# Two of eight gather passes of a graph network replaced by matmuls with an edge-count matrix

## The chip, the cores and the metric

The kernel runs on one NeuronCore of a Trainium2 chip. The metric is the device time of one execution in microseconds (us), the median of several runs. The core has five engines that run their own instruction streams and meet at semaphores: TensorE (PE in the profile, its weight loads PEld), VectorE (DVE), ScalarE (ACT), GpSimd (POOL) and SyncE (SP). DMA transfers are issued from SP, ACT and POOL queues and run on 16 DMA engines. A lower-case q behind an engine (DVEq) marks work of its instruction sequencer.

## What is computed

A graph of 6250 nodes with 128 features and 100,000 edges (sorted by destination) goes through four residual blocks, each behind a layer norm and a relu:

```
x = x + sage(relu(norm(x)))                                  # layer k=0
x = x + edge-product layer(relu(norm(x)))                    # k=1
h = relu(norm(x));  h = relu(sage(h)) twice; x = x + sage(h) # k=2, 3, 4
x = x + three attention layers(relu(norm(x)))                # k=5, 6, 7

sage(h) = mean over edges into a node of h[src] @ Wl + h @ Wr + bias
        = (segment_sum(h[src], dst) / max(count, 1)) @ Wl + h @ Wr + bias
```

The layers k=2, 3 and 4 use the same edges and no edge data, so all three sum the same neighbours; only h differs.

## The kernel before

Nodes lie in 49 tiles of 128 (X, H, G, T and acc are [128, 49*128] in SBUF, f32), handled in 13 chunks of four tiles. Edges lie in 784 tiles of 128, handled in 98 groups of eight (HT = 8); src_t holds the source node of each edge, one column a tile, and loc_t its destination as a number counted from the tile's first node.

Every layer is one pass over all edges. For an ordinary one (edge_pass, k = 0, 2, 3, 4):

- SP stores the chunks of h to one of two tables in DRAM (store_chunk, L724).
- POOL gathers: per edge tile one indirect DMA fetches 128 rows of 512 bytes from the table into rows (L839), 782 a pass. rows has space for two groups, so group c+2 waits until PE has multiplied group c.
- DVE makes, per group, a one-hot matrix from loc_t (make_onehot, L1665), [128 edges, 8, 128 ranks].
- PE multiplies each tile of rows with its one-hot into PSUM (edge_pass, L1263). The result has features on partitions and up to 128 distinct nodes of the tile as columns.
- DVE adds each result into acc at a column that depends on the data: it loads eight start columns into registers (L1674), and adds (add_group, L1689). Each add waits for the one before it.
- In the first 13 groups the product h @ Wr of each chunk is made beside it (turn_rows L1142, copy_turned L903, multiply_rows L1155, take_product L1657).
- Behind the last group, to_nodes takes acc through ACT copies (L942, L957) and two matmuls a tile (L1180 with Wl, L1188 with a permutation by rank that also divides by the count, held in G), and DVE adds the rest and applies the relu (mean_layer, L1877, L1885).

The next layer's gathers wait for the whole table (table_stored). Nothing sets the order but the program text of each engine and the semaphores. k = 1 has its own loops, and k = 5 to 7 (weighted_pass, gathers at L869, DVE's L1774, L1299 on PE) gather too; in these, DVE also picks attention terms with a register-addressed scalar column (L1969).

## Time and profile before

| | |
|---|---|
| three timed runs | 10985.27, 11006.49 and 11007.10 us, median 11006.49 us |
| profiled execution | span 8897.5 us from its first to its last instruction; no time of its own is given beside the span |
| median of the runs less the span | 2109.0 us, in no view of the profile |
| instructions in the span | 96287 |
| mean granted TensorE clock | 0.645 of full speed |
| busy share of the span | PE 49%, DVE 58%, ACT 15%, POOL 71% |
| DMA | 852.66 MB, mean 96 GB/s |

The span is what the profile's views explain. A busy share is an average over stages. The profile records an f32 matmul as two matmul records. "issue" as the reason of an idle stretch means that the engine waited for nothing that the profile shows. In a timeline, x8 stands for eight instructions that follow each other without a gap, and the number behind the start is the length of all of them.

### The profile page before, as it was taken

To read this page: it belongs to the slowest core of one execution; us is meant where nothing else is said; L and a number is where in the kernel's file an instruction comes from. 1 tells how busy PE (TensorE), PEld (TensorE's weight loads), DVE (VectorE), ACT (ScalarE), POOL (GpSimd) and SP (SyncE) were. 2 spreads that over 40 slices of the span, in tenths; PEclk is the share of its full clock that TensorE was granted. 3 is DMA by queue.
4 is the path that set the end of the run, shared out by engine and by line. 5 is a ranking of instruction groups with operands and counts; after the bars stand their busy time and mean duration, and the time that the engine had idled before them with its cause. 6 is when DMAs were issued, how large, how long until landed. Compare 5 with 4: busy or idle time off the path is not lost.

```text
span 8897.5 us, 96287 instructions
## 1 busy us (share of the span) xinstructions
PE 4351.6 (49%) x25019; PEld 3448.9 (39%) x25019; DVE 5136.5 (58%) x15655; ACT 1373.0 (15%) x2233; POOL 6316.3 (71%) x6609
## 2 busy tenths in 40 slices
PE   5565566665433344333533347454266453473533
PEld 3444433333433344333433334254243452443532
DVE  6876577776433333333433348686379773596844
ACT  6666634333100000000100010000010000100000
POOL 6777477776677767777677757777767777677774
PEclk8777777776655566556655565576565665656765
DMA  6555467775211121111221212332123331223311
GB/s 183 157 155 156 137 194 205 199 200 149 70 52 52 52 60 53 52 52 52 59 53 52 53 49 80 116 115 78 38 68 115 120 90 44 72 82 116 115 53 34
DMA packets 598959, 852.66 MB, mean 96 GB/s; under 512 B 130268, under 2 KB 404941, under 8 KB 597456
## 3 DMA queue, kind: packets, MB, share of 16 engines
q0 software_dynamic: 211168, 413.92, 18.0%
q1 hardware_dynamic: 372748, 381.31, 13.9%
q10 hardware_dynamic: 14688, 53.48, 1.5%
q8 instruction: 127, 2.08, 0.1%
q14 instruction: 228, 1.87, 0.1%
HBM read 652.71 MB, written 195.51 MB: 95 GB/s over the span
## 4 chain that ended last, share of the span: by engine, by line
POOL 70%; issue 24%; DVE 3%; PE 2%; ACT 1%; DMA 1%; SPq 0%; POOLq 0%; ACTq 0%; DVEq 0%
POOL rows L839 41%; POOL rows L869 25%; POOL nd L852 2%; POOL at_first L845 2%; PE PS L1180 1%; POOL acc L886 0%; PE PS L1188 0%; DMA rows<-table,src_t 0%; DVE moments L1615 0%; DVE H L2039 0%; DVE H L2040 0%; DVE H L2038 0%; ACT H L929 0%; DVE H L1877 0%; SPq L587 0%
## 5 line engine op out<-in xcount | busy, mean ns | idle before, releaser
L839 POOL DMA_INDIRECT rows<-table,src_t x3910 | 3728.9, 954 | 1465.9 <-issue 1257.2
L1689 DVE TENSOR_TENSOR acc<-acc,PS 128x128 f32 x5474 | 1555.2, 284 | 2914.0 <-PE PS L1263 1708.4
L869 POOL DMA_INDIRECT rows<-table,src_t x2346 | 2245.2, 957 | 903.4 <-issue 758.1
L1263 PE MATMUL PS<-onehot,rows 128*128 128x128 f32 x6256 | 1411.0, 416 | 2189.1 <-DMA rows<-table,src_t 2174.8
L1263 PEld LDWEIGHTS PS<-onehot,rows 128*128 128x128 f32 x6256 | 1306.5, 318 | 2350.8 <-DMA rows<-table,src_t 2330.2
L1299 PE MATMUL PS<-onehot,rows 128*128 128x128 f32 x3060 | 678.1, 411 | 1145.0 <-DMA rows<-table,src_t 1118.0
L1299 PEld LDWEIGHTS PS<-onehot,rows 128*128 128x128 f32 x3060 | 625.4, 312 | 1191.1 <-DMA rows<-table,src_t 1171.2
L1774 DVE TENSOR_SCALAR onehot<-PS,loc_t,shared 128x128 f32<-128x128 f32 x2346 | 942.6, 403 | 0.3
L942 ACT ACTIVATE rows<-acc 128x128 f32 x343 | 78.0, 297 | 2696.5 <-DVE acc L1689 2691.6
L1665 DVE TENSOR_TENSOR onehot<-PS,loc_t 128x1024 f32<-128x1024 f32 x392 | 476.8, 1217 | 0.6
L1372 PEld LDWEIGHTS PS<-als_bf,onehot 128*128 128x128 bf16 x7056 | 308.3, 119 | 427.4 <-DVE onehot L1957 269.7
L1969 DVE SCALAR_TENSOR_TENSOR H<-iota_row,srchi_t,PS 128x49 f32<-128x49 f32 x2352 | 456.9, 254 | 5.9 <-issue 5.9
L1372 PE MATMUL PS<-als_bf,onehot 128*128 128x49 bf16 x7056 | 347.2, 218 | 164.3 <-DVE onehot L1957 155.4
L1957 DVE TENSOR_SCALAR onehot<-PS,iota_col 128x1024 bf16<-128x1024 f32 x294 | 374.0, 1273 | 3.5 <-PE PS L1362 3.5
L1317 PE MATMUL PS<-ident,G 128*128 128x128 f32 x784 | 179.0, 404 | 316.1 <-DVE G L1805 217.9
L1095 ACT ACTIVATE small<-small 128x49 f32<-128x49 f32 x3 | 0.7, 245 | 2020.0 <-DVE small L2021 2020.0
L1362 PE MATMUL PS<-cut_row,ones_bf 1*128 1x512 bf16 x588 | 302.2, 616 | 11.4 <-DVE nd L1951 11.4
L1309 PE MATMUL PS<-H,mats 128*128 128x512 f32 x392 | 300.6, 912 | 10.5 <-DMA H<-soft_rows 10.5
L1299 PE MATMUL PS<-onehot,H 128*128 128x128 f32 x1632 | 271.8, 337 | 38.2 <-DVE onehot L1774 38.1
L1317 PEld LDWEIGHTS PS<-ident,G 128*128 128x128 f32 x784 | 143.5, 211 | 364.1 <-DVE G L1805 265.9
L1299 PEld LDWEIGHTS PS<-onehot,H 128*128 128x128 f32 x1632 | 265.9, 255 | 44.4 <-issue 44.2
L1805 DVE TENSOR_TENSOR G<-G,rows 128x1024 f32<-128x1024 f32 x98 | 120.0, 1224 | 249.4 <-DMA rows<-table,src_t 246.8
(320 smaller groups left out, 5444.5 us busy)
## 6 DMA issues: line engine op xcount, KB each, us to landing
rows<-table,src_t POOLq DMA_INDIRECT x6256, 2.9
staged<-rows ACTq DMA_DIRECT2D x102, 512.0 KB
H<-staged SPq DMA_DIRECT2D x102, 512.0 KB
soft_rows<-shared SPq DMA_DIRECT2D x196, 256.0 KB
H<-soft_rows SPq DMA_DIRECT2D x98, 512.0 KB, 3.9
prod_rows<-onehot SPq DMA_DIRECT2D x98, 512.0 KB, 5.0
shared<-in_edge_weight SPq DMA_DIRECT2D x195, 256.0 KB, 3.6
G<-in_edge_attr SPq DMA_DIRECT2D x97, 512.0 KB, 6.4
```

The source lines that it names most:

```text
L839: pool.indirect_dma_start(rows[:, h * HT + j, :], None, table[k % 2], at(src_t[:, t:t + 1]))\
L869: pool.indirect_dma_start(rows[:, g % 2 * HT + j, :], None, table[k % 2], at(src_t[:, t:t + 1]))\
L1263: last = mm(window_at(k, c, j), rows[:, r, :], onehot[:, r, :], start=True, stop=True)
L1299: last = mm(PS[:, o:o + D], block[:, j * D:(j + 1) * D], onehot[:, h * HT + j, :], start=True, stop=True)
L1317: last = tr(PS[:, 2048 + j * D:2048 + (j + 1) * D], msg0[:, j * D:(j + 1) * D], ident[:])
L1362: last = mm(bank(q), ones_bf[0:1, :], lo_row[:, q * 512:(q + 1) * 512], start=True, stop=True)
L1372: last = mm(PS[:, o:o + NT], hot_bf[:, h, j, :], als_bf[:, part * NT:(part + 1) * NT], start=(part == 0), stop=(part == 2))
L1665: tt(onehot[:, h * HT:(h + 1) * HT, :], iota_ps.unsqueeze(1).broadcast_to([P, HT, D]), loc_t[:, t:t + HT].unsqueeze(2).broadcast_to([P, HT ...
L1689: tt(at, at, window_at(k, c, j), ALU.add).then_inc(added[h], 1 if j < n - 1 else HT - n + 1)
L1774: return ts(onehot[:, c % 2 * HT + j, :], iota_ps, loc_t[:, t:t + 1], ex_t[:, t:t + 1], ALU.is_equal, ALU.mult)
L1957: ts(hot_bf[:, h, :, :].rearrange("p a b -> p (a b)"), PS[:, h * 1024:(h + 1) * 1024], iota_col[:], None, ALU.is_equal).then_inc(lo_hot[h], 1)
L1969: last = stt(mask[:, j, :], iota_row[:, 0:NT], srchi_t[:, ds(e, 1)], cand[:, j, :], ALU.is_equal, ALU.mult, accum_out=als_t[:, ds(e, 1)])
```

## The change

The layers k = 3 and k = 4 no longer gather (GATHERED = 0, 1, 2, 5, 6, 7; DENSE = 3, 4). Their neighbour sums are matmuls of h with a matrix of edge counts A[src, dst] in f32, kept in DRAM as 98 slabs of 64 destination nodes, each [128, 49*64] (adjacency, 98 x 3136 words a partition, which is 157.4 MB).

The matrix is made during the gather pass of k = 2. The 784 edge tiles and the 784 windows of eight destination nodes are walked together in 1567 steps, one edge tile and one window in each. For a step DVE writes two bf16 matrices: the low 7 bits of the source as one-hot [128, 128], and a mask [128, 392] that is 1 at (source tile, node in window) of the edge. PE opens the target with a 4-column matmul and multiplies the two ([128, 392], bf16) into one of three PSUM banks, adding to what the window has so far, and ACT copies the whole window (49 runs of eight words) into one of two slabs in H after every step. SP stores a finished slab. Which tile, bank and slab a step uses depends on the data: the numbers are worked out by DVE and PE in groups 2 to 11 of the pass (compare_tiles, count_tiles, plan_steps, plan_stores) and loaded into registers 16 (DVE, ACT) or 32 (PE) at a time. The steps begin in group 14 and are spread evenly over the 84 groups left. In this pass PE uses three banks for the edge windows, as in k = 0.

```diff
+DENSE = (3, 4);  GATHERED = (0, 1, 2, 5, 6, 7)
+WN = 8;  MASKW = NT * WN;  WINDOWS = ET;  STEPS = ET + WINDOWS - 1
+SLABW = 64;  SLABS = WINDOWS * WN // SLABW;  SLAB_WORDS = NT * SLABW
+LOAD_REGS = 16;  STEP_FROM = 14;  LEAD = 6;  RING = 8
+UNIT_TILES = 7;  UNITS = NT // UNIT_TILES;  SLOTS = 4
...
# SP
+            def store_slabs():
+                sp.wait_ge(tables_ready, 1)
+                for q in range(SLABS):
+                    done = sp.value_load(sp_table[:, q:q + 1], min_val=9, max_val=STEPS + 1)
+                    sp.wait_ge(evacuated, done)
+                    sp.wait_ge(slabs_moved, 16 * (q + 1))
+                    sp.dma_start(adjacency[:, q * SLAB_WORDS:(q + 1) * SLAB_WORDS], slab(q)).then_inc(slabs_moved, 16)
...
+            def load_units(k):
+                for c in range(NCH):
+                    for u in range(UNITS):
...
+                        elif n >= SLOTS:
+                            sp.wait_ge(units_used, n - SLOTS + 1)
...
+                        sp.dma_start(slot_of(n)[:, 0:nslabs(c)],
+                                     of[:, :, u * UNIT_TILES:(u + 1) * UNIT_TILES, :]).then_inc(units_in[n % SLOTS], 16)
...
# POOL
-            for k in range(K):
+            for k in GATHERED:
...
# ACT
+            def evacuate(i, first):
+                s.wait_ge(stepped, i)
+                s.wait_ge(evacuated, i)
+                to = H[:, ds(first[WN + i % WN], SLAB_WORDS)].rearrange("p (h d) -> p h d", d=SLABW)[:, :, 0:WN]
+                nc.scalar.activation(to, PS[:, ds(first[i % WN], MASKW)].rearrange("p (h d) -> p h d", d=WN), ACT.Copy)\
+                    .then_inc(evacuated, 1)
...
# PE
+            def adjacency_step(i):
+                if i % LOAD_REGS == 0:
+                    pe.load(bank_regs, pe_table[:, 2 * i:2 * (i + LOAD_REGS)])
...
+                wait(pe, evacuated, i - 1)
+                pe.wait_ge(masked, i + 1)
+                mm(PS[:, ds(bank_at[LOAD_REGS + i % LOAD_REGS], 4)], ones_bf[:], zeros_bf[:, 0:4], start=True, stop=True)
+                mm(PS[:, ds(bank_at[i % LOAD_REGS], MASKW)], lo_slot(i), mask_slot(i), start=False, stop=True,
+                   skip_group_check=True).then_inc(stepped, 1)
...
+                        for i in range(steps_by(c - 1), steps_by(c)):
+                            adjacency_step(i)
...
+            def dense_pass(k):
...
+                            last = mm(sums_at(c).rearrange("p (s d) -> p s d", d=SLABW), of[:, t, :],
+                                      slot_of(n)[:, 0:nslabs(c), j, :], start=(t == 0), stop=(t == NT - 1))
+                        last.then_inc(units_used, 1)
...
+                for c in range(NCH):
+                    wait(pe, sums_copied, done + c - 1)
+                    add_units(c, range(0, 2))
+                    turn_rows(k, c)
+                    if c > 0:
+                        means(c - 1)
+                    add_units(c, range(2, 4))
+                    multiply_rows(k, c)
+                    add_units(c, range(4, UNITS))
+                means(NCH - 1)
...
# DVE
+            def mask_step(i):
+                if i % LOAD_REGS == 0:
+                    v.load(tile_regs, dve_table[:, i:i + LOAD_REGS])
...
+                wait(v, stepped, i - RING + 1)
+                ts(lo_slot(i), iota_16[:, 0:D], slo_t[:, ds(t, 1)], None, ALU.is_equal)
+                ts(mask_slot(i), iota_16[:, 0:MASKW], window_cols[:, i:i + 1], key_t[:, ds(t, 1)], ALU.add, ALU.is_equal)\
+                    .then_inc(masked, 1)
...
+                    begun, ended = steps_by(c - 1), steps_by(c)
+                    if c >= STEP_FROM:
+                        masks_to(begun + LEAD)
+                        add_group(2, c, c * HT,
+                                  lambda j: masks_to(begun + LEAD + (ended - begun - LEAD) * (j + 1) // HT))
+                        masks_to(ended)
```

means(c) multiplies the sums of chunk c, copied to SBUF by ACT, with Wl; dense_layer on DVE multiplies with 1/count, adds the product h @ Wr and the bias, and applies the relu (k = 3) or adds x and takes the moments for the next norm (k = 4), chunk by chunk. A unit is [128, 8 slabs, 7 source tiles, 64], 1.84 MB in runs of 1792 bytes; a full chunk needs seven, the last chunk has two slabs instead of eight.

How the pass of k = 2 changes on the engines, in the middle of the pass. DVE before, one group of edges (from the load of the start columns to the one-hot of group c+2):

```order
L1674 TENSOR_LOAD seg_row
L1675 ISA
L1689 ISA [waits added1,multiplied0]
L1689 TENSOR_TENSOR acc<-acc,PS 128x128
L1689 ISA [waits added0]
L1689 TENSOR_TENSOR acc<-acc,PS 128x128
```

and DVE now, the same place (L1925 is the add, L2068 the one-hot of the source, in bn, and L2069 the mask, in shared or cut_row):

```order
L1925 ISA [waits added1]
L1925 TENSOR_TENSOR acc<-acc,PS 128x128
L2068 ISA [waits stepped]
L2068 TENSOR_SCALAR bn<-work,shared 128x128
L2069 ISA
L2069 TENSOR_SCALAR shared<-work,GT,shared 128x392
L2068 ISA [waits stepped]
L2068 TENSOR_SCALAR bn<-work,shared 128x128
L2069 ISA
L2069 TENSOR_SCALAR shared<-work,GT,shared 128x392
```

Between two adds there now stand two or three steps of two operations each, and each step waits until PE has done the one eight before.

PE now, at the seam between the steps of one group and the edge matmuls of the next (L1452 is the line that was L1263, RO the rows and one-hots); before, only the rows of L1263 stood here:

```order
L1432 MATMUL PS<-cut_row,bn 128x392
L1452 MATMUL PS<-RO 128x128 [waits added1,onehot_ready1,gathered1]
L1452 MATMUL PS<-RO 128x128 x3
L1452 MATMUL PS<-RO 128x128 [waits added0]
L1452 MATMUL PS<-RO 128x128 x3
L1431 ISA [waits masked,evacuated]
L1431 MATMUL PS<-work,ones_bf 128x4
L1432 ISA
L1432 MATMUL PS<-cut_row,bn 128x392
L1431 ISA [waits masked,evacuated]
```

The eight edge matmuls of a group stand in one block, and no step runs on PE while they do.

ACT now, where it takes up the next eight steps (ACT had no instruction in this part of the pass before):

```order
L1099 ACTIVATE H<-PS 128x49x8
L1108 TENSOR_LOAD GT
L1109 ISA
L1110 ISA
L1111 TENSOR_LOAD GT
L1111 ISA x2
L1099 ISA [waits evacuated,stepped,slabs_moved]
L1099 ACTIVATE H<-PS 128x49x8
L1099 ISA [waits evacuated,stepped]
```

Every copy waits for its own predecessor (evacuated) and for PE (stepped); every eighth has two register loads before it, and a wait for a stored slab.

Listed row by row (rows that repeat folded), the five engines' programs have 24195 rows before and 37593 now.

## Rows read from the trace of the kernel before

**Rows 1.** Page: the chain that ended last, shares of the span by engine.

```profile
POOL 70%; issue 24%; DVE 3%; PE 2%; ACT 1%; DMA 1%; SPq 0%; POOLq 0%; ACTq 0%; DVEq 0%
```

**Rows 2.** Chain in order of time (start, length): table stores before k = 2, 3, 5.

```profile
2256.16 2.10 DMA table<-H
...
3276.87 1.93 DMA table<-H
...
5349.09 2.32 DMA table<-H
```

**Rows 3.** Timeline of k = 3 from 3511.8 us (start, length, engine, line).

```profile
3511.81 3.78 PE L1263 MATMUL PS<-onehot,rows 128*128 128x128 f32 x16 [6.19 <-DMA rows<-table,src_t]
3513.01 0.94 POOL L839 DMA_INDIRECT rows<-table,src_t  x1 [0.30 <-issue]
...
3515.72 3.22 DVE L1689 TENSOR_TENSOR acc<-acc,PS 128x128 f32 x8 [5.61 <-PE PS L1263]
...
3518.86 1.22 DVE L1665 TENSOR_TENSOR onehot<-PS,loc_t 128x1024 f32<-128x1024 f32 x1
...
3521.86 3.78 PE L1263 MATMUL PS<-onehot,rows 128*128 128x128 f32 x16 [6.26 <-DMA rows<-table,src_t]
```

**Rows 4.** Stages (start:end, us, busy of PE, PEld, DVE, ACT, POOL, clock, DMA share, GB/s).

```profile
3244.00:3279.00 35.00, 27.22 (x208) 26.47 (x208) 18.16 (x39) 18.43 (x62) 0.95 (x1) 0.84 0.34 96
3279.00:4265.00 986.00, 383.21 (x1700) 357.04 (x1700) 345.71 (x883) 7.44 (x13) 736.96 (x782) 0.60 0.20 52
```

**Rows 5.** Groups by line and shape: ScalarE PSUM copy, VectorE scalar op in SBUF.

```profile
L957 ACT ACTIVATE onehot<-PS 128x512 f32<-128x512 f32 x84 | 49.7, 592 | 30.4 <-PE PS L1180 30.3
...
L1003 ACT ACTIVATE H<-PS,bias_cols 128x1024 f32<-128x1024 f32 x98 | 109.3, 1115 | 613.5 <-PE PS L1309 613.5
...
L1885 DVE TENSOR_SCALAR H<-H 128x512 f32<-128x512 f32 x24 | 10.2, 426 | 0.8
```

**Rows 6.** Register loads (8 and 4 registers) and register arithmetic: ns min/median/max.

```profile
L1674 DVEq TENSOR_LOAD <-seg_row x686: 593/596/1094, 61.1 to 8816.8; - x172
...
L1675 DVEq FUSED_REGOPS  x686: 157/189/195, 62.0 to 8817.5; - x172
...
L938 ACTq TENSOR_LOAD <-rank_row x91: 293/310/912, 1050.2 to 8842.5; - x91
```

**Rows 7.** Timeline, TensorE at the end of k = 7 and its loads at 303 us.

```profile
8825.47 1.06 PE L1188 MATMUL PS<-onehot,G 128*128 128x128 f32 x8
8826.36 1.06 PE L1180 MATMUL PS<-gat_wa,rows 128*128 128x128 f32 x8
...
303.69 0.19 PEld L1247 LDWEIGHTS PS<-shared,mats 128*128 128x128 f32 x1 [0.24 <-issue]
304.12 0.19 PEld L1247 LDWEIGHTS PS<-shared,mats 128*128 128x128 f32 x1 [0.24 <-issue]
```

**Rows 8.** Timeline, VectorE in k = 5: adds and weights in turn, then picks.

```profile
5984.09 0.40 DVE L1774 TENSOR_SCALAR onehot<-PS,loc_t,shared 128x128 f32<-128x128 f32 x1
5984.41 0.28 DVE L1689 TENSOR_TENSOR acc<-acc,PS 128x128 f32 x1
...
5440.48 0.25 DVE L1969 SCALAR_TENSOR_TENSOR H<-iota_row,srchi_t,PS 128x49 f32<-128x49 f32 x1
...
5440.67 0.25 DVE L1969 SCALAR_TENSOR_TENSOR H<-iota_row,srchi_t,PS 128x49 f32<-128x49 f32 x1
```

**Rows 9.** Timeline, gathers and VectorE casts within SBUF in k = 0.

```profile
102.91 1.30 POOL L839 DMA_INDIRECT rows<-table,src_t  x1 [0.30 <-issue]
106.13 0.94 POOL L839 DMA_INDIRECT rows<-table,src_t  x1 [0.30 <-issue]
...
102.83 0.57 DVE L1493 CAST G<-G 128x784 bf16<-128x784 f32 x1
```

**Rows 10.** DMA from 1500 to 1520 us: GB/s in 40 slices of 0.5 us, packets.

```profile
GB/s 66 229 360 373 327 347 353 283 277 335 349 268 104 16 131 0 131 0 0 238 66 139 401 346 343 348 389 295 296 327 365 288 117 0 131 0 41 90 0 131
DMA packets 4957, 4.15 MB, mean 208 GB/s; under 512 B 354, under 2 KB 4450, under 8 KB 4957
```

More of the change, by code:

```diff
@@ L79 @@
 SAGE = (0, 2, 3, 4)
+DENSE = (3, 4)
 GAT = (5, 6, 7)
+GATHERED = (0, 1, 2, 5, 6, 7)
+WN = 8
+MASKW = NT * WN
+WINDOWS = ET
+STEPS = ET + WINDOWS - 1
+SLABW = 64
+SLABS = WINDOWS * WN // SLABW
+SLAB_WORDS = NT * SLABW
+LOAD_REGS = 16
+PLAN_FROM = 2
+STEP_FROM = 14
+LEAD = 6
+RING = 8
+UNIT_TILES = 7
+UNITS = NT // UNIT_TILES
+UNIT_WORDS = CW * UNIT_TILES
+SLOTS = 4
+PLANS = -(-(STEPS + 1) // PW)
 def build(nc, a, out):
@@ L1721, in edge_pass, with edge_keys @@
                         first_softplus(p)
+            def edge_keys():
+                dst8, digit, own, first = (scan_tmp(G, i) for i in range(4))
+                v.wait_ge(slabs_moved, 16)
+                step(ts(dst8.bitcast(I32), key_t.bitcast(I32), 3, None, ALU.arith_shift_right))
+                step(ts(digit.bitcast(I32), key_t.bitcast(I32), WN - 1, None, ALU.bitwise_and))
+                step(copy(own, digit.bitcast(I32)))
+                step(copy(first, dst8.bitcast(I32)))
+                step(stt(own, srchi_t[:], float(WN), own, ALU.mult, ALU.add))
+                step(stt(key_t, first, 512.0, own, ALU.mult, ALU.add))
+                step(ts(digit.bitcast(I32), src_t[:], P - 1, None, ALU.bitwise_and))
+                step(copy(slo_t, digit.bitcast(I32)))
@@ new lines, in compare_tiles @@
+            def compare_tiles(p):
+                w = plan_width(p)
+                for b in range(NB):
+                    if p < PLANS:
+                        last = ts(compared(b)[:, 0:w], iota_16[0:TB, 0:w], float(p * PW), tile_end[:, b:b + 1],
+                                  ALU.add, ALU.is_gt)
+                    else:
+                        last = ts(compared(b)[:, 0:w], iota_16[0:TB, 0:w], 8.0, tile_window[:, b:b + 1],
+                                  ALU.mult, ALU.is_gt)
+                step(last, tiles_compared)
@@ new lines, in plan_stores, with plan @@
+            def plan_stores():
+                v.wait_ge(edges_counted, PLANS + 1)
+                sums = only_last
+                row = int_a[0:1, 0:SLABS].bitcast(F32)
+                step(stt(row, iota_16[0:1, 0:SLABS], 8.0, counted_ps[0:1, 0:SLABS], ALU.mult, ALU.add))
+                step(ts(sp_table, row, 9.0, None, ALU.add), tables_ready)
+            def plan(c):
+                if c == 0:
+                    edge_keys()
+                if c == 1:
+                    step_constants()
+                p, rest = divmod(c - PLAN_FROM, 2)
+                if 0 <= p <= PLANS:
+                    if rest == 0:
+                        compare_tiles(p)
+                    elif p < PLANS:
+                        plan_steps(p)
+                    else:
+                        plan_stores()
@@ new lines, in gather_and_build, with masks_to @@
+            def gather_and_build():
+                made = 0
+                def masks_to(n):
+                    nonlocal made
+                    while made < min(n, STEPS):
+                        mask_step(made)
+                        made += 1
+                for c in range(2):
+                    make_onehot(c)
+                for c in range(NG):
+                    begun, ended = steps_by(c - 1), steps_by(c)
[4 more added lines that the diff above has]
+                        masks_to(ended)
+                    else:
+                        add_group(2, c, c * HT)
+                    if c + 2 < NG:
+                        make_onehot(c + 2)
+                    if 1 <= c <= NCH:
+                        take_product(2, c - 1)
+                    plan(c)
@@ new lines, in dense_layer @@
+            def dense_layer(k):
+                done = (k - 3) * NCH
+                for c in range(NCH):
+                    g, x = chunk(acc3 if k == 3 else H3, c), chunk(X3, c)
+                    v.wait_ge(means_ready, done + c + 1)
+                    step(tt(g, as_tiles(means_at(c)), per_node(rcount, c), ALU.mult), means_used)
+                    v.wait_ge(p_product, c + 1 + k * NCH)
+                    tt(g, g, as_tiles(product_at(k, c)), ALU.add).then_inc(p_done, 1)
+                    v.wait_ge(p_done, c + 1 + k * NCH)
+                    step(tt(g, g, vec_nodes(bias_vec[k], len(tiles_of(c))), ALU.add))
+                    if k == 3:
+                        ts(g, g, 0.0, None, ALU.max).then_inc(h_chunks, 1)
+                    else:
+                        step(tt(x, g, x, ALU.add))
+                        row_moments(c)
+                        if c > 0:
+                            shift_rows(c - 1, False)
+                if k == 4:
+                    shift_rows(NCH - 1, False)
```

341 lines of the change are left out of this document (278 added, 63 removed).

## The prediction

> **What bounds the kernel now.** I read the page first. The chain that ended last is POOL for 70% of the span and "issue" for 24% [rows 1]; the reader is to see that no arithmetic engine is in it. The chain in order of time gives the layers' borders, each the landing of the last table chunk [rows 2]: k = 2 runs from 2258.3 to 3278.8 us, 1020.5 us, and k = 3 and 4 together to 5351.4 us, 2072.6 us. Then the timeline inside a pass [rows 3]: a gather is 0.94 us and the next starts 0.30 us later, so a group of eight takes 10.0 us, which is the distance from one TensorE block to the next (3511.81 to 3521.86). In those 10 us TensorE is busy 3.78 us, and DVE 3.22 for the adds and 1.22 for a one-hot. The stages [rows 4] say the same: of the 986 us pass, PE is busy 383, DVE 346, ACT 7, at a granted clock of 0.60. A pass is 98 groups at the pace of POOL, and the others have room beside it.
>
> **What goes.** Two gather passes with their node stages: 2072.6 us.
>
> **What comes in the pass of k = 2.** 1567 steps over 84 groups are 18.65 a group. They are free while each engine's work for a group stays under 10.0 us. I price the engines in turn.
>
> ACT copies 128x392 from PSUM per step. Copies of 512 and 1024 columns took 592 and 1115 ns [rows 5], so about 1.02 ns a column, and 392 make 0.47 us. Each copy waits for its own predecessor before its addresses are made. The adds do the same: eight take 3.22 us and one 0.28 [rows 3, 8], so 0.42 from start to start and 0.14 of it wait. A step is 0.61 us. Every eighth step first loads 16 registers: 8 cost 596 ns and 4 cost 310 [rows 6], so 72 each and 1.17 us for 16; with the arithmetic on them (0.19 for eight, twice), a 17th register and its arithmetic (0.2) it is 1.75 us, of which the copy still running covers 0.47. That leaves 1.3 in eight steps: 0.77 us a step, **14.4 us a group**. Already this is above 10.0.
>
> To it comes the seam. PE's block of eight edge matmuls runs 3.78 us at the low clock [rows 3] and 1.8 us at the high one (four matmuls in 0.89 us [rows 7]); I take 2.8, since the clock was granted to 0.60 [rows 4] and PE will be somewhat busier. When PE turns to the block, ACT has three copies left, 1.8 us. Block, last step and first new step (0.3 us each, from their columns at the high clock) are 3.4 us, so ACT idles 1.6 us. PE's own load of 32 registers (2.3 us, and 0.8 of arithmetic) comes each 16 steps, but ACT has three copies and its own load then, also 3.1 us: nothing. Sum: 16.0 us.
>
> DVE. The picks, whose operand column comes from a register too, follow each other every 0.19 us [rows 8]: a floor of 0.37 us for a step's two operations. The ceiling is one element a cycle with the fixed part of L1774 (0.32 us for 128 columns [rows 8]): 0.32 and 0.60, so 0.92. An operation within SBUF ran faster: 512 columns of four bytes in 426 ns [rows 5] where one a cycle would need 533. If it is bytes that count, the mask's 392 two-byte columns stream in 0.10 us; with 0.19 fixed for each, the pair costs 0.47, which I take as it stands nearest to this row and to the floor. A group is then 8.8 plus eight adds (2.2), one-hot (1.2) and register loads (2.6): 14.8 us. The Trainium skill (VectorE: DVE Perf Modes, "The perf-mode tier table") gives 16-bit scalar operations within SBUF four elements a cycle; no row here shows one, and by it the sum would be the same.
>
> PE: block 2.8, steps about 0.4 each (7.5) and loads 3.6: 13.9 us. POOL: gathers get longer while DVE works within SBUF. Two gathers that met a 0.57 us cast took 1.30 us, not 0.94 [rows 9]: 0.36 more, 0.63 of the cast's length. Of a group's 8.8 us of masks that is 5.5 us, so 15.5 with the 10.0.
>
> The Trainium skill has the rule for it (SBUF — State Buffer, "Who interferes with whom"): two-port VectorE operations and GpSimd exclude each other for the whole instruction. The trace agrees in kind, with 0.36 us of the 0.57; held in full, it is a rival below.
>
> So four chains need 16.0, 15.5, 14.8 and 13.9 us for a group and hand work to each other through rings of three to eight steps. I take **16.5 us**, half a microsecond for their friction, between 13.0 (no load exposed) and 18.8.
>
> The layer k = 2: 14 groups at 10.0 (140); 20 us for the planning in groups 2 to 11 (some 100 small DVE operations of about 0.4 us, mostly beside the gathers; the ends are 0 and 50); 84 x 16.5 = 1386; the node stage, 35 as before [rows 4], and 8 for the last copy and the last slab's store. Together 1589 us, 568 more than before. SP's stores (98 of 1.6 MB) fill the DMA engines only in part: 157 MB in 1.4 ms is 113 GB/s, beside 50 for the gathers.
>
> **What comes as k = 3 and 4.** A full chunk is 49 matmuls of 512 columns. An f32 matmul is two records, and two records of 512 columns start 0.43 us apart [rows 7], so 0.86 us for a matmul; twelve chunks make 506 us. The last chunk of 128 columns takes 49 x 0.22 = 11, and turn, product and means (three more of 128 columns for 49 tiles) 33. That is 550 us at the high clock. Whether it is held: through the end of k = 7 [rows 7] PE ran without a gap at 0.89 us for eight records, the high level; in the passes, with gaps of 6.2 us before each block, a block took 3.78, the low level [rows 3]. A dense layer has no gaps as long as units arrive. A unit is 1.84 MB for seven matmuls, 6.0 us, so 306 GB/s are asked. With 4450 of 4957 packets under 2 KB the engines moved 277 to 401 GB/s in the slices in which they were hardly idle [rows 10]; a unit's 1792-byte runs should do no worse: 5.3 us at the 345 in the middle, and 6.6 at 277, which would make a layer 50 us longer. Four slots cover the rest. I add 10 us a layer for gaps, 8 for the first units, and 15 behind the last chunk until the table of k = 5 has landed (the norm is made chunk by chunk beside the sums). 2 x 560 + 23 = 1143 us, 929.6 less than the 2072.6.
>
> **Sum.** Span 8897.5 + 568 - 930 = 8536 us. Between the span and the runs' median lie 2109 us that no view explains; I leave them as they are, so 11006.5 - 361 = **10645 us**, -3.3%. A change under about 0.2% could not be told from none.
>
> **Rivals.**
> - VectorE sets the pace. At two elements a cycle, as the row of 426 ns has it, a step costs 0.64 and a group 11.9 + 6.0 = 17.9 us: 84 x 1.4 more, 10763 us. At one a cycle 23.2 us, +563: 11208 us, slower. For it: mask operations have two column operands, and L1774 is such. Against: the operations in SBUF show better than one. 0.17, of it 0.05 for the second.
> - POOL sets the pace. If gathers lose the masks' full length, 10.0 + 8.8 = 18.8 us a group, +193: 10838 us. It needs the exclusion to be whole, where rows 9 show 0.36 of 0.57. The rule of the Trainium skill (SBUF — State Buffer, "Who interferes with whom") is this case. 0.12.
> - The other side: units come too slowly in k = 3 and 4. At 200 GB/s, a little under the 208 that rows 10 moved with their idle slices, a unit takes 9.2 us, a layer 793, and the result is 11111 us; if the gaps also drop TensorE to the low level, a matmul takes 1.71 us, a layer 1100, and the result is 11725. It decides from 8.6 us a unit (213 GB/s) on, where the two layers give back the 361. Against it: the full slices of rows 10. For it: the slabs lie 12.5 KB apart within a row, and no row shows such a read. 0.11.
> - It does not do what it says: the 2109 us around the span grow. The programs have 37593 rows and not 24195; if that time goes with them, it grows by 1168 to some 11810 us. No view shows it either way. 0.05.
> - The forecast keeps 0.55, between 10350 (13.0 us groups: 84 x 3.5 less) and 10900.
>
> **Chances.** Faster: the forecast 0.55, VectorE at two a cycle 0.12, POOL 0.12 together 0.79; within 0.2%: 0.03, from the milder end of slow units; slower: 0.18, from slow units (0.08), VectorE at one a cycle (0.05) and the time around (0.05). The range reaches from 10300, a little under the 13.0 us groups, to 11100, which takes in both pace rivals and slow units at their start; the one-a-cycle masks, cold dense layers and a grown surrounding are left out.
>
> **What would show it.** Right: k = 2 takes about 1590 us, with steps of about 0.77 us on ACT beside idle time of 1.6 us a group before the first copy; TENSOR_LOAD on ACT near 1.17 us; PE in k = 3 and 4 at a clock over 0.95, 0.43 us between records, hardly waiting for units. Wrong: POOL without pauses in k = 2 and gathers of 2 us; DVE over 90% busy there; PE in k = 3 waiting for units; or a span that falls while the runs don't.

## The result: slower by 3.2%, and the profile after

| | |
|---|---|
| changed kernel, four runs | 11346.44 to 11361.01 us, median 11352.08 us |
| kernel before, four runs | 10981.07 to 11007.10 us, median 10995.88 us |
| ratio | 1.0321, 95% interval 1.0306 to 1.0335 |
| predicted | 10645 us (10300 to 11100) |
| profiled execution of the changed kernel | 11347.99 us, span 11346.2 us, TensorE clock 0.643 |

The time lies outside the range and on the other side of no change. The first thing to see is the last row: here span and time differ by 2 us. There are no 2109 us around the span, as there seemed to be in the kernel before; experiment e0 takes that up.

Page of the changed kernel: busy shares, three rows of the 40 slices, and the chain (which answers to [rows 1]).

```profile
PE 5627.2 (50%) x27414; PEld 3519.3 (31%) x27414; DVE 5247.5 (46%) x17197; ACT 2131.4 (19%) x3703; POOL 4841.9 (43%) x5045
...
POOL 5666466655222222221000173266570466650664
PEclk7766666666555555556999955566555665555756
...
GB/s 163 136 133 140 141 162 172 162 146 49 81 80 81 81 74 81 85 82 111 297 284 291 238 79 36 52 98 41 56 95 6 93 72 36 75 72 19 101 59 34
...
DVE 2%; POOL 2%; issue 2%; another core or an unknown queue 1%; PE 0%; DVEq 0%; DMA 0%; POOLq 0%; ACT 0%; SPq 0%
```

The chain can't be followed back in this execution (its shares sum to 7%), so the passes have to be measured by their gathers. In the slices, POOL falls to 2 tenths for eight slices (the pass of k = 2), and then TensorE's clock stands at 9 tenths and the DMA engines at 238 to 297 GB/s for four (k = 3 and 4). The second is what was predicted, the first is not.

Changed kernel, POOL's gathers of k = 2 and the first of k = 5: count, duration in ns (min/median/max), first and last start in us.

```profile
L958 POOL DMA_INDIRECT RO<-table,src_t x782: 939/947/1305, 2647.4 to 5258.9; - x196
```

```profile
L988 POOL DMA_INDIRECT RO<-table,src_t x24: 943/947/948, 6470.2 to 6498.9; - x24
```

The pass of k = 2 takes 2612 us (5258.9 + 0.95 - 2647.4), where 140 + 20 + 1386 = 1546 were forecast. From its last gather to the first of k = 5 it is 1210 us, where 43 + 1143 = 1186 were forecast. The dense layers are nearly right and the building of the matrix is not.

Changed kernel, two stages (columns as in [rows 4]): the middle of the pass of k = 2, and the dense layers.

```profile
2800.00:5200.00 2400.00, 1090.50 (x4270) 562.73 (x4268) 958.61 (x3699) 734.38 (x1477) 620.71 (x654) 0.57 0.22 80
5500.00:6000.00 500.00, 495.96 (x1391) 238.90 (x1390) 30.08 (x56) 13.70 (x24) 0.00 (x0) 1.00 0.83 287
```

In the pass nobody is busy for half of the time, so it is no engine's throughput. In the dense layers PE is busy 496 of 500 us at the high clock, with 287 GB/s beside it.

What the pass waits for stands in the timeline at a sixteenth step. Changed kernel, from 3990.7 us (rows of POOL, PEld and most of the others left out):

```profile
3990.82 0.50 PE L1432 MATMUL PS<-cut_row,bn 128*128 128x392 bf16 x1
...
3991.45 0.50 ACT L1099 ACTIVATE H<-PS  x1 [0.19 <-issue]
...
3998.61 0.50 ACT L1099 ACTIVATE H<-PS  x1 [6.66 <-issue]
...
4001.94 0.18 PE L1431 MATMUL PS<-work,ones_bf 3*128 3x4 bf16 x1 [10.62 <-issue]
...
4002.73 0.25 DVE L2068 TENSOR_SCALAR bn<-work,shared 128x128 bf16<-128x128 int16 x1 [8.43 <-PE PS L1432]
...
4002.99 0.50 ACT L1099 ACTIVATE H<-PS  x1 [3.89 <-PE PS L1432]
```

PE stands for 10.6 us and ACT for 6.7, both for "issue", and DVE and ACT then wait for PE. The register loads of this run say why (line 1427 is PE's load of 32 registers, 1108 and 2064 those of 16 on ACT and DVE, 1910 the load of eight start columns that was at L1674; the three numbers are the shortest, the median and the longest, in ns):

```profile
L1427 PEldq TENSOR_LOAD <-GT x98: 7516/10073/10575, 2822.4 to 5305.9; - x98
```

```profile
L1108 ACTq TENSOR_LOAD <-GT x196: 3367/3392/6607, 2809.0 to 5319.4; - x196
```

```profile
L2064 DVEq TENSOR_LOAD <-GT x98: 3582/3594/4121, 2817.9 to 5297.1; - x98
```

```profile
L1910 DVEq TENSOR_LOAD <-seg_row x490: 593/597/1756, 61.4 to 11266.2; - x164
```

By the medians that is 315 ns a register on PE, 212 on ACT and 225 on DVE, where [rows 6] gave 72 to 78. The load of seg_row is still at 75 in this same execution, so it isn't the execution that makes loads slow. The new tables hold 16-bit numbers (`G[0:1, ...].bitcast(U16)`); seg_row and rank_row, on which the price rested, hold 32-bit ones.

### The profile page after: what moved, and what is told of

Same layout as the page of the kernel before. It is cut to its first block and busy times, and to the rows that moved or that the text cites. A ratio compares the mean times of both kernels' runs of the same rounds, so it can differ in the third digit from the quotient of the medians.

```text
span 11346.2 us, 113568 instructions
## 1 busy us (share of the span) xinstructions
PE 5627.2 (50%) x27414; PEld 3519.3 (31%) x27414; DVE 5247.5 (46%) x17197; ACT 2131.4 (19%) x3703; POOL 4841.9 (43%) x5045
## 3 DMA queue, kind: packets, MB, share of 16 engines
q0 software_dynamic: 161120, 311.32, 10.6%
## 5 line engine op out<-in xcount | busy, mean ns | idle before, releaser
L988 POOL DMA_INDIRECT RO<-table,src_t x2346 | 2256.6, 962 | 3367.4 <-DMA table<-H 1287.9
L958 POOL DMA_INDIRECT RO<-table,src_t x2346 | 2242.8, 956 | 2919.5 <-PE PS L1452 1676.6
L1925 DVE TENSOR_TENSOR acc<-acc,PS 128x128 f32 x3910 | 1098.0, 281 | 1674.0 <-remote 1074.8
L1530 PE MATMUL PS<-RO 128*128 128x128 f32 x3060 | 649.1, 398 | 1136.7 <-DMA RO<-table,src_t 776.2
L1099 ACT ACTIVATE H<-PS x1567 | 779.4, 497 | 1716.3 <-issue 977.6
L1603 PE MATMUL PS<-als_bf,RO 128*128 128x49 bf16 x7056 | 397.4, 218 | 1192.5 <-issue 903.2
L1530 PEld LDWEIGHTS PS<-RO 128*128 128x128 f32 x3060 | 602.3, 301 | 1182.8 <-DMA RO<-table,src_t 797.3
L2169 DVE TENSOR_SCALAR RO<-PS,loc_t,shared 128x128 f32<-128x128 f32 x2346 | 943.4, 404 | 0.6
L2068 DVE TENSOR_SCALAR bn<-work,shared 128x128 bf16<-128x128 int16 x1567 | 411.2, 262 | 1123.0 <-PE PS L1432 792.4
L1452 PE MATMUL PS<-RO 128*128 128x128 f32 x3128 | 593.5, 366 | 182.7 <-DMA RO<-table,src_t 97.2
L1452 PEld LDWEIGHTS PS<-RO 128*128 128x128 f32 x3128 | 579.9, 279 | 288.1 <-DMA RO<-table,src_t 132.0
L1490 PE MATMUL PS<-GT,H 128*128 128x512 f32 (+1 forms) x966 | 394.1, 565 | 1.4 <-DMA GT<-adjacency 1.4
L1490 PE MATMUL PS<-GT,acc 128*128 128x512 f32 (+1 forms) x952 | 392.3, 569 | 0.0
```

Of the source, the lines that this page charges most:

```text
L958: pool.indirect_dma_start(rows[:, h * HT + j, :], None, table[k % 2], at(src_t[:, t:t + 1]))\
L988: pool.indirect_dma_start(rows[:, g % 2 * HT + j, :], None, table[k % 2], at(src_t[:, t:t + 1]))\
L1099: nc.scalar.activation(to, PS[:, ds(first[i % WN], MASKW)].rearrange("p (h d) -> p h d", d=WN), ACT.Copy)\
L1452: last = mm(window_at(k, c, j), rows[:, r, :], onehot[:, r, :], start=True, stop=True)
L1490: last = mm(sums_at(c).rearrange("p (s d) -> p s d", d=SLABW), of[:, t, :], slot_of(n)[:, 0:nslabs(c), j, :], start=(t == 0), stop=(t == N ...
L1530: last = mm(PS[:, o:o + D], block[:, j * D:(j + 1) * D], onehot[:, h * HT + j, :], start=True, stop=True)
```

## The experiments

The kernel before took about 11000 us in some sets of runs and about 8900 in others, so every time below is compared only with the kernel before of its own set. Beside e0 it took 11058.56, beside e1 to e4 8902.85, beside e5 and e6 11061.59, beside e7 to e9 8905.75 us. Passes are given from the first gather to the end of the last. e0, e2, e3, e4 and e9 were run once, the others four times.

### e0: the kernel before, once more

No edit.

> The kernel before, unchanged, profiled once more. The profile on record has a span of 8897.5 us where its timed runs take 11006, while the changed kernel's profile (11346 us) agrees with its runs (11348). Theory 1 (the profiled execution of before was not like the timed ones: something slows every pass of the timed runs that was absent from it): the new span is about 10990 us, and the gather pass of k = 2 takes longer than 1020 us, about 1300. Theory 2 (2109 us of work lie around the span, in this kernel alone): the new span is again about 8900 us beside a time of about 11000.

Measured: 11036.5 us with a span of 11034.6. The kernel before, this execution: the gathers of k = 2, and the first of k = 5.

```profile
L839 POOL DMA_INDIRECT rows<-table,src_t x782: 938/944/958, 2649.9 to 3765.4; - x196
```

```profile
L869 POOL DMA_INDIRECT rows<-table,src_t x45: 940/944/953, 6136.9 to 6198.8; - x45
```

So the missing 2109 us are inside the span. The profile from which the forecast was made was of an execution of the 8900 kind, while the runs beside it were of the 11000 kind. In e0 the pass of k = 2 takes 1116 us, not 987 (and not the 1300 or so that Theory 1 had guessed), with each gather as long as before (944 ns), and the three layers k = 2 to 4 take 3487.0 us (6136.9 - 2649.9) where the record has 3093.2 (5351.7 - 2258.5 by the same two lines). Most is lost in k = 5 to 7: from their first gather to the end of the span it is 4898 us and not 3546. The same kernel, TensorE's attention work in k = 5 with gathers beside it, and after they have stopped:

```profile
6300.00:6560.00 260.00, 18.41 (x88) 8.05 (x87) 10.64 (x67) 0.00 (x0) 195.78 (x195) 0.50 0.32 98
6620.00:6880.00 260.00, 192.18 (x2322) 105.78 (x2320) 250.38 (x1545) 0.00 (x0) 0.00 (x0) 0.50 0.03 11
```

and the execution on which the prediction was made, with gathers beside the same work:

```profile
5500.00:5760.00 260.00, 133.25 (x1587) 72.99 (x1584) 200.79 (x1093) 0.00 (x0) 197.37 (x200) 0.50 0.35 112
```

With the same 195 to 200 gathers beside it TensorE gets through 88 records in one case and 1587 in the other, and the profile gives "issue" for most of its idle time in the first; once the gathers pause, it gets through 2322. What differs between the two kinds of set was not found.

### e1: tables of 32 bits

```diff
-        pe_table = G[0:1, 1568:2 * 1568].bitcast(U16)
-        act_table = G[0:1, 2 * 1568:2 * 1568 + 2352].bitcast(U16)
-        dve_table = G[0:1, 2 * 1568 + 2352:2 * 1568 + 2352 + 784].bitcast(U16)
+        pe_table = G[0:1, 1568:3 * 1568].bitcast(I32)
+        act_table = G[32:33, 1568:4 * 1568].bitcast(I32)
+        dve_table = G[0:1, 3 * 1568:4 * 1568].bitcast(I32)
```

> The three tables that PE, ACT and DVE load registers from hold 32-bit numbers instead of 16-bit ones (ACT's lies on partition 32, since the row of partition 0 is full); nothing else is changed. Theory A (the loads are dear because the numbers are 16 bits wide: seg_row, 32 bits, costs 75 ns a register, these tables 212 to 315): PE's load of 32 registers falls from 10.07 us to about 2.4, ACT's and DVE's of 16 from 3.39 and 3.59 to about 1.2, so 16 steps lose 7.7 us on PE and 4.4 on ACT; the group goes from 29 us to about 17, the pass of k = 2 from 2612 us to about 1650, and the time from 11352 to about 10400. Theory B (a register costs 200 to 300 ns when 16 or more are loaded at once, or from this part of SBUF, whatever their width): nothing changes, 11350. Theory C (VectorE or the port shared with POOL sets the pace of the pass and the loads lie beside it): loads may fall, but the time stays above 11200.

Measured: 8689.33 us beside 8902.85, ratio 0.9762 (0.9746 to 0.9778): now faster than the kernel before. The loads, and the gathers of k = 2:

```profile
L1427 PEldq TENSOR_LOAD <-GT x98: 2127/2132/3876, 2412.6 to 3978.7; - x98
```

```profile
L1108 ACTq TENSOR_LOAD <-GT x196: 1004/1022/2604, 2397.2 to 3988.0; - x196
```

```profile
L2064 DVEq TENSOR_LOAD <-GT x98: 1095/1100/1930, 2407.5 to 3972.2; - x98
```

```profile
L958 POOL DMA_INDIRECT RO<-table,src_t x782: 938/944/1667, 2253.4 to 3951.0; - x196
```

64 to 69 ns a register, on all three engines, and a pass of 1699 us in place of 2612 (2595 in this kind of set, e8); the forecast of Theory A was 1650. Theory B (count or place) is out, since count and tile are the same, and C (VectorE or the port) too: nothing on DVE or POOL but the load of DVE was changed.

### e2: a 32-bit table for TensorE alone

```diff
-        pe_table = G[0:1, 1568:2 * 1568].bitcast(U16)
-        act_table = G[0:1, 2 * 1568:2 * 1568 + 2352].bitcast(U16)
-        dve_table = G[0:1, 2 * 1568 + 2352:2 * 1568 + 2352 + 784].bitcast(U16)
+        pe_table = G[0:1, 1568:3 * 1568].bitcast(I32)
+        act_table = G[32:33, 1568:1568 + 2352].bitcast(U16)
+        dve_table = G[0:1, 3 * 1568:3 * 1568 + 784].bitcast(U16)
```

> Only PE's table holds 32-bit numbers; ACT's lies on partition 32 with its 16 bits. Theory A: PE's load is about 2.4 us, ACT's still 3.4 and DVE's 3.6; of the 11 us that PE stood before every sixteenth step some 7.5 go, so a group is about 20 to 22 us and the time about 10750 to 10950, two thirds of the way to the kernel with all three tables changed. Theory B: 11350. If a load from partition 32 is dearer or cheaper than one from partition 0, ACT's median shows it here apart from the width.

Measured: 9239.08 us beside 8902.85. The numbers of the expectation were for a set of the 11000 kind; in this set the changed kernel takes 9609 (e8) and e1 8689, so TensorE's table, changed first, is worth 370 of the 920 us, and not two thirds; the other 550 come with the tables of ACT and DVE, which no run changes apart. The pass takes 2229 us. ACT's load from partition 32, and two of its copies at a load:

```profile
L1108 ACTq TENSOR_LOAD <-GT x196: 3367/3412/6550, 2409.3 to 4542.6; - x196
```

```profile
3511.92 0.50 ACT L1099 ACTIVATE H<-PS  x1 [7.11 <-issue]
...
3521.24 0.50 ACT L1099 ACTIVATE H<-PS  x1 [4.02 <-issue]
```

3412 ns for 16-bit numbers on partition 32, beside 3392 on partition 0 and 1022 for 32-bit ones on partition 32 (e1): between these two partitions it makes no difference, the width does. And where ACT has a load, it stands for 4 us or more, each eighth step.

### e3: no steps

```diff
-                    done = sp.value_load(sp_table[:, q:q + 1], min_val=9, max_val=STEPS + 1)
-                    sp.wait_ge(evacuated, done)
+                    g = STEP_FROM + q * (NG - 2 - STEP_FROM) // SLABS
+                    sp.wait_ge(multiplied[g % 2], g // 2 + 1 + turn[2] * ITERS)
...
-                    evacuations()
...
-                        for i in range(steps_by(c - 1), steps_by(c)):
-                            adjacency_step(i)
...
-                    if c >= STEP_FROM:
+                    if c >= NG:
                         masks_to(begun + LEAD)
```

> The 1567 steps are left out (no masks, no step matmuls, no ACT copies); planning, the stores of the 98 slabs (paced by the groups) and the dense layers stay. The neighbour sums of k = 3 and 4 are then made with what happens to lie in H. Theory A and B alike: the pass of k = 2 runs at the pace of the kernel before in its own timed runs (1117 to 1151 us), with up to 50 more for the slab stores beside the gathers; so the time is about 11352 - 2612 + 1150 = 9890 us, and the dense layers still take 1210 us from the last gather of k = 2 to the first of k = 5. Rival: the stores of 157 MB slow the gathers by themselves (the pass over 1300 us, the time over 10050).

Measured: 7940.68 us beside 8902.85. Gathers of k = 2, the first of k = 5, and half a millisecond of the dense layers:

```profile
L958 POOL DMA_INDIRECT RO<-table,src_t x782: 938/944/1303, 2260.4 to 3262.5; - x196
```

```profile
L988 POOL DMA_INDIRECT RO<-table,src_t x18: 940/944/947, 4397.7 to 4418.9; - x18
```

```profile
3300.00:3800.00 500.00, 498.44 (x1326) 233.84 (x1325) 25.35 (x42) 13.56 (x23) 0.00 (x0) 1.00 0.86 298
```

The expected total was for the other kind of set; in this one the comparison is the pass itself. It takes 1003 us, 16 more than before the change, with planning and all 98 slab stores in it. The forecast had 20 us for the planning alone, and the rival of this run (stores slow the gathers) is out. From the last gather of k = 2 to the first of k = 5 it is 1134 us, 76 less than with the steps. The first dense matmuls say where these lie, in e3 and in the changed kernel:

```profile
L1487 PE MATMUL PS<-GT,H x966: 273/592/697, 3298.8 to 3843.3; 128*128 128x512 f32 x177, 128*128 128x128 f32 x17
```

```profile
L1490 PE MATMUL PS<-GT,H x966: 272/592/697, 5368.6 to 5912.8; 128*128 128x512 f32 x177, 128*128 128x128 f32 x17
```

Without steps the first comes 35 us behind the last gather, which is the node stage of the forecast; with them it comes 109 us behind it: the last copy of ACT starts at 5329.3 us, 69 us behind the last gather, and the last slab is stored behind that. The forecast had 43 for this, and 8 for the first units. From the first dense matmul to k = 5 it is 1099 and 1102 us, where 1135 were left.

### e4: the same steps at fixed addresses

```diff
-                        s.load(evac_regs, act_table[:, at:at + 2 * WN])
...
-                        freed = s.value_load(act_table[:, at + 2 * WN:at + 2 * WN + 1], min_val=16, max_val=16 * SLABS)
+                        ws = [(j + 1) // 2 for j in range(i, i + WN)]
+                        first = [((w + 3) & 3) * 512 + 3 * 512 for w in ws]
...
-                    pe.load(bank_regs, pe_table[:, 2 * i:2 * (i + LOAD_REGS)])
...
+                    ws = [(j + 1) // 2 for j in range(i, i + LOAD_REGS)]
...
-                    v.load(tile_regs, dve_table[:, i:i + LOAD_REGS])
...
+                    tile_at[:] = [j // 2 for j in range(i, i + LOAD_REGS)]
```

> Every step takes its tile, bank and slab from constants as if edge tiles and windows alternated, so that no register is loaded or computed for a step; the masks, matmuls, copies and stores have the same number and size as in the changed kernel, but the counts are of the wrong edges. Theory A and B: with all loads gone the pace is that of ACT's copies, 0.69 us a step (0.50 and the gap behind it), 12.9 us a group, and 3 us of seam: 16 us, the pass about 1500 us, the time about 10250. If register arithmetic in the address of each operation matters too, steps are shorter than 0.69 us and the pass nears 1300. Theory C (masks or the port): the pass stays above 2000 us and the time above 10750.

Measured: 8246.58 us beside 8902.85. Gathers of k = 2, and ACT's copies in the pass (16 in 9.38 us):

```profile
L958 POOL DMA_INDIRECT RO<-table,src_t x782: 938/945/1304, 2258.7 to 3536.6; - x196
```

```profile
2999.73 9.38 ACT L1099 ACTIVATE H<-PS 128x392 f32<-128x392 f32 x16
```

The pass takes 1279 us, below the 1500 of the expectation and near the 1300 that it had for the case in which register addresses cost too: a copy at a constant address starts 0.59 us after the one before it, where it was 0.69 at a register's. So the register address costs 0.10 us a copy, up to 157 us in the 1567 of them. Of the 420 us between e1 and this kernel, 263 or more are the loads together with the register arithmetic of PE and DVE, which this run leaves out at once. All masks, matmuls, copies and stores are here, and a group takes (1279 - 140)/84 = 13.6 us: neither VectorE at one element a cycle (23.2 us) nor POOL losing the masks' length (18.8) can be. ACT makes up the whole group: behind each block of edge matmuls it has stood for 2.5 us, and 18.65 copies at 0.59 are 11.0.

```profile
3011.65 10.56 ACT L1099 ACTIVATE H<-PS 128x392 f32<-128x392 f32 x18 [2.53 <-PE PS L1431]
```

(The windows lie in four PSUM banks; the text ahead of the prediction says three. No term rests on it.)

### e5 and e6: the changed kernel and the one with 32-bit tables, side by side

No new edit.

> The changed kernel, unaltered. The kernel before took 11006 us in the first runs and 8903 beside e1 to e4, so the same program differs by 2100 us between two sets of runs, and the changed kernel has to be timed in the same set as the one with 32-bit tables. If the set is again of the 8900 kind: the pass of k = 2 takes 2612 us as before (its pace is set by register loads, and those lasted the same in both), so the time is 8689 - 1699 + 2612 = 9600 us, 7 to 8% over the kernel before, and not 3%. If it is of the 11000 kind: 11350 again. Rival: a good part of the 2612 us was of the same kind as the 2100 us; then the pass is near 2200 and the time near 9200.

> The kernel of e1 (32-bit tables), unaltered. In a set of the 8900 kind: 8690, ratio 0.976. In a set of the 11000 kind: the pass of k = 2 was 2612 us with 16-bit tables; 32 bits take about 910 us off it, so 11352 - 910 = 10440 us, ratio 0.95. Rival for that kind: the pauses that make the kernel before slower there stretch this pass too (more instructions on PE and ACT than any other pass), and it comes out over 10700.

Measured, in a set of the 11000 kind: the changed kernel 11397.29 us beside 11061.59, ratio 1.0306 (1.0289 to 1.0323); with 32-bit tables 10637.87 us, ratio 0.9616 (0.9600 to 0.9632). Gathers of k = 2 in e6:

```profile
L958 POOL DMA_INDIRECT RO<-table,src_t x782: 942/947/1679, 2669.7 to 4552.1; - x196
```

1883 us, where e1 had 1699: in this kind of set the pass that is paced by engines is stretched as the gather passes are, and e6 comes out 200 us over its expectation, though under its rival's 10700.

### e7: loads where an engine waits anyway

```diff
+                        if k == 2 and c > STEP_FROM and j in (2, 5):
+                            b = -(-steps_by(c - 1) // WN)
+                            b += b in banks_at
+                            if b not in banks_at and b * WN < steps_by(c):
+                                load_banks(b)
...
+                        if i in seams and i // WN + 1 not in evac_at and (i // WN + 1) * WN <= STEPS:
+                            load_evac(i // WN + 1)
```

(load_banks loads 16 registers of PE for eight steps, load_evac 16 of ACT; both write to another set than the one in use.)

> 32-bit tables as in e1, and the loads placed where the engine waits anyway: PE loads 16 registers for eight steps instead of 32 for sixteen, up to two such loads in the middle of the block of edge matmuls; ACT loads one set of 16 early, when it is about to wait for the first step behind the block. Theory A: of the 420 us that e1's pass of k = 2 has over the one without any loads (1699 against 1279), PE's share (some 1.7 us of ACT idle time 98 times) mostly goes, and ACT's for one of its 2.3 loads a group (84 times 1.2): 150 to 250 us less than e1's pass, so 1450 to 1550 us and a time of 8440 to 8540 beside a kernel before of 8903 (ratio 0.95 to 0.96); in a set of the 11000 kind about 10400. Rival: PE's sequencer doesn't run ahead of its matmuls, so that a load in the block lengthens the block by its 1.1 us, and the pass stays within 50 us of e1's.

Measured: 8638.27 us beside 8905.75, ratio 0.9699 (0.9682 to 0.9715), the fastest version that leaves nothing out; it is 51 us below e1 (43 below e9, of its own set), not 150 to 250. The pass takes 1649 us. TensorE at a block of edge matmuls with a load in it, and the loads:

```profile
3202.98 1.49 PE L1466 MATMUL PS<-RO 128*128 128x128 f32 x6
3205.55 2.82 PE L1466 MATMUL PS<-RO 128*128 128x128 f32 x10 [1.08 <-issue]
```

```profile
L1436 PEldq TENSOR_LOAD <-GT x196: 1100/1105/3472, 2418.5 to 3935.2; - x196
```

Behind the third edge matmul (six records) TensorE stops for 1.08 us, the length of the load. The sequencer had not run far enough ahead to cover it, and the rival holds. ACT's idle time in front of its copies is 749.7 us here and 799.2 in e1, so the gain is there; whether it comes from ACT's earlier loads or from PE's shorter ones, the runs do not tell apart. The expectation was also too high for a reason of its own: the 1.7 us that it gave to PE's load are the pause that ACT makes for its own. In e1, at an eighth step without a load of PE, and at one with it:

```profile
3010.69 0.50 ACT L1099 ACTIVATE H<-PS  x1 [1.69 <-issue]
...
3018.29 0.50 ACT L1099 ACTIVATE H<-PS  x1 [2.31 <-issue]
```

So PE's load of 2.13 us adds 0.6 us to ACT's pause, 60 us in 98 of them, and not 170.

### e8 and e9: the changed kernel in a set of the 8900 kind

No new edit.

> The changed kernel, unaltered, a third time, to have it beside e7 and e9, and if the set is of the 8900 kind, for the first time in such a set: then 9600 us, ratio 1.08; in one of the 11000 kind 11390 again, ratio 1.03.

> The kernel of e1 and e6, to have one look of it in this set: 8690 us if the kernel before takes 8900, 10640 if it takes 11060.

Measured: the changed kernel 9609.45 us beside 8905.75, ratio 1.0790 (1.0772 to 1.0808); with 32-bit tables 8681.47. Changed kernel, gathers of k = 2 and TensorE's loads:

```profile
L958 POOL DMA_INDIRECT RO<-table,src_t x782: 938/945/1304, 2264.9 to 4859.0; - x196
```

```profile
L1427 PEldq TENSOR_LOAD <-GT x98: 7520/10073/10593, 2423.9 to 4906.0; - x98
```

The pass takes 2595 us here and 2612 in the first runs, and a load 10073 ns in both. The pass that waits for 16-bit loads costs nearly the same in both kinds of set, and so do the dense layers (1210 us from the last gather of k = 2 in both); the gather passes do not. So the change loses 7.9% where the gather passes that it replaces run undisturbed, and 3.1 to 3.2% where they are slow themselves.

## Why the prediction was wrong

| stretch | forecast | 11000 kind | 8900 kind | 32-bit tables, 8900 kind |
|---|---|---|---|---|
| pass of k = 2 | 1546 | 2612 | 2595 | 1699 |
| its last gather to the first of k = 5 | 1186 | 1210 | 1210 | 1183 |
| k = 2 to 4 before | 3093 | 3487 | 3093 | 3093 |
| difference | -361 | +336 | +712 | -212 |
| measured difference of the medians | | +356, +336 | +704 | -214 |

(The columns are from the gathers of the first profile after and e0, of e8, and of e1, where k = 5 starts at 6070.5 and 5135.1 us; the 3093 before is that of the record in both of the last.) Between first gather of k = 2 and first of k = 5 lies all that the change does.

**The step that failed** is the price of a register: "8 cost 596 ns and 4 cost 310 [rows 6], so 72 each and 1.17 us for 16", and "2.3 us" for PE's 32. They measured 3.39 and 10.07 us. The rows were sound, and e1 gives 64 to 69 ns for 32-bit numbers from the same tile; the forecast applied them to tables of 16-bit numbers. The width stands in the change (`bitcast(U16)`), and in none of the diff lines that I chose to work from. That the width is the cause is shown by e1 and e2; why it is so dear is not. By the shortest loads of the changed kernel and of e1, 16 bits cost 3.3 to 3.5 times as much on all three engines (ACT 3367 and 1004 ns, DVE 3582 and 1095, PE 7516 and 2127). The rest of PE's 10.07 us is not in the width alone: ACT's load is mostly near 3.4 us, and often about 6.0 where PE loads at the same time. The forecast had no term for loads that meet, and no run separates it.

**"Nothing" for PE's load** failed with it. It was to hide behind three copies of ACT and ACT's own load, 3.1 us. In the timelines above ACT has one copy left when PE turns away. At 32 bits the term is small all the same, 0.6 us in sixteen steps (e7's rows of e1). At 16 bits ACT stands for 6.66 and 3.89 us around PE's load, 10.55 together, where its own load alone costs it 4.03:

```profile
3986.65 0.50 ACT L1099 ACTIVATE H<-PS  x1 [4.03 <-issue]
```

ACT's idle time in front of its copies is 1716 us in the first profile after (1567 copies):

```profile
L1099 ACT ACTIVATE H<-PS x1567 | 779.4, 497 | 1716.3 <-issue 977.6
```

**The pace of ACT otherwise**: a step was to be 0.61 us and is 0.69 (0.50 for the copy, 0.19 behind it). With 32-bit loads the group is (1699 - 140)/84 = 18.6 us, where 16.5 were forecast in a range of 13.0 to 18.8. The chain that was named as the bound is the right one (e4, where ACT's copies and its pause at the block make up the group), and the total of e1, 214 us below its kernel before, keeps the sign of the forecast and 0.6 of its size.

**DVE** was priced nearly right. The masks, changed kernel:

```profile
L2068 DVE TENSOR_SCALAR bn<-work,shared x1567: 235/249/510, 2822.2 to 5318.7; 128x128 bf16<-128x128 int16 x196
```

```profile
L2069 DVE TENSOR_SCALAR shared<-work,GT,shared x784: 367/376/535, 2822.3 to 5317.2; 128x392 bf16<-128x392 int16 x196
```

From 128 to 392 columns it is 127 ns, 0.48 ns a column: about two in the time that the forecast called a cycle (533 ns for 512), if both operations have the same fixed part. They are not the same operation, since the mask has a second column operand, so the rate is not shown. The rule of the Trainium skill (VectorE: DVE Perf Modes, "The perf-mode tier table") of four 16-bit elements a cycle would leave 69 of the 127 ns to the columns, an estimate from that page's rate and the forecast's cycle; the rows neither show it nor exclude it. In the full run a pair takes 0.55 us from start to start (4002.73 to 4003.28 us), where 0.47 were taken. The rival that put VectorE at two a cycle may have the rate, and has not the consequence: with no loads (e4) the group is 13.6 us, and DVE doesn't set it.

**POOL**: 5.5 us a group of lost gather time was wrong. In the pass a gather takes 947 ns in the median with masks beside it, and 944 without (e3). The better test is e4, where the masks' lengths sum to 824 us in the 900 from 2600 to 3500 us (483 and 341, with some overlap). POOL's gathers in the same 900 us:

```profile
2600.00:3500.00 900.00, 508.25 (x528) 0.68 0.49 176
```

That is a mean of 963 ns a gather, so about 0.15 us a group is lost. What [rows 9] showed beside a cast between f32 and bf16 did not come back beside 16-bit masks. The exclusion of the Trainium skill (SBUF — State Buffer, "Who interferes with whom") is stated there for VectorE's two-port modes; the gathers show none of it, and whether the masks ran in such a mode is not shown.

**The dense layers** came out nearly as worked out, 1102 us against 1135 (see e3), and the 1210 against 1186 from gather to gather hide two errors of opposite sign: up to the first dense matmul it took 109 us, not 51, since the steps end 70 us behind the gathers. In the layers PE is busy 496 of 500 us at the high level of 2.4 GHz, 287 GB/s. The unit loads, changed kernel:

```profile
GT<-adjacency SPq DMA_DIRECT2D x126, 1792.0 KB, 7.2
```

7.2 us from issue to landing, within four slots of 6.0 us each. The other side was given to this rival (slow units) and to VectorE, together most of the 0.18 for slower; neither is what made it slower.

**"I leave them as they are"**, of the 2109 us around the span, was wrong as a reading and left 394 us out of the sum: in such runs the kernel before takes 3487 us for k = 2 to 4, not 3093. By luck this error is opposite to the other, and hides a part of the miss: on the numbers of the profile alone the forecast was off by 712 + 361 = 1073 us, and the runs on record show only 717 of it.

The range failed because 13.0 and 18.8 us a group were drawn from engines' work alone. A load price that no row showed for these tables should have had bounds of its own; as an estimate, at twice the price the loads of ACT and PE add 2.7 us each (2.33 times 1.17, and 1.17 times 2.3) to the 16.0, and 21.4 us a group is 84 x 4.9 = 412 us more than the forecast's 16.5, already slower than before.

## What to carry to other kernels

Look at the element type of a table before taking a price for its register loads: one that is read by several engines, some hundred times, is worth its double size in 32-bit words (here 920 us for three lines). A load on an in-order engine has to be costed against everyone who waits for that engine, and a few instructions in its queue need not cover it: here the load in the middle of a matmul block opened a gap of its own length. Check that a profile is of the same kind as the timed runs, by setting its span beside their time, before a sum rests on it; a difference of a fifth is a finding, and no constant.

## What was not expected of the hardware

- A register load from SBUF costs 64 to 78 ns a register for 32-bit numbers on PE, ACT and DVE, and by the medians 212 (ACT), 225 (DVE) and 315 ns (PE; 235 in the shortest) for 16-bit ones; on ACT, partition 0 and partition 32 gave the same. The Trainium skill (Runtime: NRT & Kernel Launch, "Instruction fetch mechanics") has about 200 ns a register for a register load, even a bulk one; that page speaks of loads from HBM. The 16-bit rows of ACT and DVE come near its figure, the 32-bit rows show a third.
- An ACT copy of 392 columns with register addresses starts 0.69 us after its predecessor, one with constants 0.59 (each waits for the one before).
- The same program takes 8900 us in some sets of runs and 11000 in others. In the slower, TensorE's small matmuls come at 88 records in 260 us while gathers run, and at 2322 when they don't; the pass paced by 16-bit loads is not touched (2595 and 2612 us), the one with 32-bit loads is (1699 and 1883). The cause was not found, and no run was made to isolate it.
